# Rotary turning of queries and keys: one projection read twice by VectorE instead of two projections

## The reference, cut to what matters

```python
q, k, v = (heads(wq, bq), heads(wk, bk), heads(wv, bv))   # x @ w.T + b, split into 16 heads of 8
xr, xi = (t[..., :half], t[..., half:])                   # half = 4
q_or_k = jnp.concatenate([xr * cos - xi * sin, xr * sin + xi * cos], axis=-1)
att = softmax(where(causal, q @ k.T / sqrt(8), -inf))
y = (att @ v) @ wp.T + bp
```

## Time and profile before

| | |
|---|---|
| median of 3 runs | 1955.2 us |
| the profiled execution | 1959.13 us |
| its span, first to last instruction | 1957.4 us |
| mean granted TensorE clock | 0.977 of full speed |
| TensorE busy | 1787.4 us (91% of the span) |
| VectorE busy | 1570.6 us (80%) |
| ScalarE busy | 1274.1 us (65%) |
| GpSimd busy | 1049.5 us (54%) |
| chain of waits, by engine | TensorE 54%, VectorE 30%, ScalarE 10% |

### The profile page before, as it was taken

One profiled execution on the slowest core, in us unless ns is written; L12 is line 12 of the kernel. 1 busy time (PEld: TensorE's weight loads), 2 busy tenths in 40 slices (PEclk: granted clock), 3 DMA queues, 4 the chain that ended last, 5 costly groups with the idle time before them and its releaser, 6 DMA issues.

```text
span 1957.4 us, 32660 instructions
## 1 busy us (share of the span) xinstructions
PE 1787.4 (91%) x11328; PEld 894.7 (46%) x11328; DVE 1570.6 (80%) x2936; ACT 1274.1 (65%) x2803; POOL 1049.5 (54%) x1124
## 2 busy tenths in 40 slices
PE   4878999999999999999999999999999999998894
PEld 2343545445454544545455454544545454453443
DVE  6487888889888798988879788887978888797661
ACT  1547577675857768586775857667585766758461
POOL 1416374665637466463746646374664647555533
PEclk8989999999999999999999999999999999999887
DMA  2211011110101111110111111011110101100000
GB/s 78 62 43 33 12 39 39 45 39 31 47 12 40 38 45 39 31 44 15 39 39 45 38 31 36 22 39 39 44 40 31 31 28 39 39 11 21 1 11 6
DMA packets 87361, 66.61 MB, mean 34 GB/s; under 512 B 10592, under 2 KB 82976, under 8 KB 87200
## 3 DMA queue, kind: packets, MB, share of 16 engines
q1 hardware_dynamic: 87200, 64.52, 10.8%
HBM read 30.42 MB, written 8.39 MB: 20 GB/s over the span
## 4 chain that ended last, share of the span: by engine, by line
PE 54%; DVE 30%; ACT 10%; issue 3%; POOL 1%; DMA 1%; SPq 0%; POOLq 0%; PEld 0%; DVEq 0%; PEldq 0%; ACTq 0%
PE Y L494 9%; DVE nmaxA L877 7%; DVE ztmp L992 6%; PE S1c L433 5%; PE S2a L459 4%; PE S1b L433 4%; DVE nmaxF L882 4%; ACT Pq L721 4%; PE S2b L459 4%; PE Y L485 4%; PE M L587 3%; PE M L545 3%; ACT PT L706 3%; DVE ztmp L964 2%; PE M L599 2%
## 5 line engine op out<-in xcount | busy, mean ns | idle before, releaser
L1110 POOL TENSOR_TENSOR Z<-Z,ztmp 128x1280 f32<-128x1280 f32 x112 | 324.6, 2898 | 339.9 <-DVE ztmp L992 338.8
L1077 POOL TENSOR_SCALAR_AFFINE_SELECT PT<-PT 128x256 f32<-128x256 f32 (+1 forms) x640 | 256.3, 410 | 290.9 <-ACT PT L706 285.8
L1101 POOL TENSOR_TENSOR Vf<-Vf,ztmp 128x512 f32<-128x512 f32 x256 | 349.0, 1363 | 94.4 <-DVE ztmp L964 85.8
L706 ACT ACTIVATE PT<-S2a 128x512 f32<-128x512 f32 x320 | 191.8, 599 | 132.5 <-PE S2a L453 126.1
L494 PE MATMUL Y<-PT,Vf 128*64 128x512 f32 x1024 | 267.8, 614 | 0.0
L710 ACT ACTIVATE PT<-S2a 128x512 f32<-128x512 f32 x256 | 153.4, 599 | 151.5 <-PE S2a L459 148.1
L964 DVE TENSOR_TENSOR ztmp<-xv,wv_s 128x512 f32<-128x512 f32 x256 | 240.2, 938 | 2.8 <-POOL Z L1110 2.8
L433 PE MATMUL S1c<-Kf,Qf 64*128 64x512 f32 x352 | 201.8, 654 | 26.8 <-ACT Pq L721 25.7
L433 PE MATMUL S1a<-Kf,Qf 64*128 64x512 f32 x352 | 201.4, 652 | 25.6 <-ACT Pq L721 25.6
L706 ACT ACTIVATE PT<-S2b 128x512 f32<-128x512 f32 x320 | 191.9, 600 | 25.9 <-PE S2b L453 25.6
L433 PE MATMUL S1b<-Kf,Qf 64*128 64x512 f32 x320 | 183.3, 653 | 10.2 <-ACT Pq L721 10.1
(11 more groups left out here) (111 smaller groups left out, 3729.8 us busy)
## 6 DMA issues: line engine op xcount, KB each, us to landing
Qs<-parts SPq DMA_DIRECT2D x96, 128.0 KB
Ks<-parts SPq DMA_DIRECT2D x96, 128.0 KB
tab_s<-in_tab SPq DMA_DIRECT2D x16, 512.0 KB, 4.4
out_x<-res SPq DMA_DIRECT2D x32, 256.0 KB, 2.2
xr<-out_x SPq DMA_DIRECT2D x24, 256.0 KB, 2.9
wa_s<-in_wa SPq DMA_DIRECT2D x16, 320.0 KB, 3.2
xl<-in_x SPq DMA_DIRECT2D x8, 256.0 KB, 3.0
Qs<-mrowA SPq DMA_DIRECT2D x128, 4.0 KB, 1.7
```

What stands on the lines that cost most here:

```text
L706: nc.scalar.activation(PT[:, slot % 2, b, :], t[:, :], ACT.Exp, scale=SCALE_A).then_inc(exps_done.sem, 1)
L1101: nc.gpsimd.tensor_tensor(Vf[:, i, :, :], Vf[:, i, :, :], vtmp[:, n % VBUF, :, :], ALU.add).then_inc(v_acc.sem, 1)
L1110: nc.gpsimd.tensor_tensor(Z[:, :, :, :], Z[:, :, :, :], ztmp[:, hh % 2, :, :, :], ALU.add).then_inc(z_acc.sem, 1)
```

## The change

The second projection of the query and of the key, `A qp` and `A kp`, goes, with its weights, its bias and its places in the list of M0. `wa_s` has 3 blocks of weights instead of 5 (the transfer goes from 320 to 192 KB). For half 1 VectorE reads the one projection again, crosswise: partitions 64 to 127 of the bank are written to partitions 0 to 63 of `rot2`, and 0 to 63 to 64 to 127, in two instructions of 64 partitions and 512 columns each. The sign in the second table moves to the other half, since it is now read on the partition of the source. The bank is given back behind the second of these, and not behind half 0; a new semaphore `turned` counts the other two instructions, and the sum waits for it. The steps stay: half 0 of the query at (2, 6), both crosswise instructions and the sum at (2, 7); of the key at (3, 5) and (3, 6).

```diff
@@ the lists of banks @@
                    "rows2", "F k2", "ZT1", "F out",
-                   "rows3", "A xnT", "A qp",
-                   "A kp", "F k3",
+                   "rows3", "A xnT",
+                   "F k3",
@@ TensorE @@
-                    w = ("A q", "A qp", "A k", "A kp").index(use)
+                    w = ("A q", "A k").index(use)
...
                         if at == (2, 6):
                             a_project("A q")
-                        if at == (2, 7):
-                            a_project("A qp")
                         if at == (3, 4):
                             a_project("A k")
-                            a_project("A kp")
@@ VectorE, rotate(qk, half) @@
-                    use = (("A q", "A qp"), ("A k", "A kp"))[qk][half]
+                    use = ("A q", "A k")[qk]
...
                     dve.wait_ge(*filled(j, use))
-                    nc.vector.scalar_tensor_tensor((rot, rot2)[half], bank(use)[:, :],
-                                                   ba_s[:, 2 * qk + half:2 * qk + half + 1], tab_s[:, half, :],
-                                                   ALU.add, ALU.mult).then_inc(is_free(use), 1)
-                    if half:
-                        for use in (("A q", "A qp"), ("A k", "A kp"))[qk]:
-                            dve.wait_ge(*drained(j, use))
-                        nc.vector.tensor_tensor(rot, rot, rot2, ALU.add).then_inc(rot_ready.sem, 1)
+                    t = bank(use)
+                    if half == 0:
+                        nc.vector.scalar_tensor_tensor(rot, t[:, :], ba_s[:, qk:qk + 1], tab_s[:, 0, :],
+                                                       ALU.add, ALU.mult).then_inc(turned.sem, 1)
+                        return
+
+                    nc.vector.scalar_tensor_tensor(rot2[0:P // 2, :], t[P // 2:P, :], ba_s[P // 2:P, qk:qk + 1],
+                                                   tab_s[P // 2:P, 1, :], ALU.add, ALU.mult).then_inc(turned.sem, 1)
+                    nc.vector.scalar_tensor_tensor(rot2[P // 2:P, :], t[0:P // 2, :], ba_s[0:P // 2, qk:qk + 1],
+                                                   tab_s[0:P // 2, 1, :], ALU.add, ALU.mult).then_inc(is_free(use), 1)
+                    dve.wait_ge(turned.sem, turned.at(j, 2 * qk + 2))
+                    dve.wait_ge(*drained(j, use))
+                    nc.vector.tensor_tensor(rot, rot, rot2, ALU.add).then_inc(rot_ready.sem, 1)
@@ the host @@
-        w = np.stack([wq[:, plain], wq[:, swapped], wk[:, plain], wk[:, swapped], wv], 1)
-        b = np.stack([bq[plain], bq[swapped], bk[plain], bk[swapped]], 1)
+        w = np.stack([wq[:, plain], wk[:, plain], wv], 1)
+        b = np.stack([bq[plain], bk[plain]], 1)
...
-        tabs.append(np.stack([np.repeat(np.concatenate([cos, cos]), H, 0), np.repeat(np.concatenate([-sin, sin]), H, 0)], 1))
+        tabs.append(np.stack([np.repeat(np.concatenate([cos, cos]), H, 0), np.repeat(np.concatenate([sin, -sin]), H, 0)], 1))
```

More of the change, by code:

```diff
@@ L96, in attention_and_mixture @@
         maskb = sb("maskb", [P, P], BF)
-        wa_s = sb("wa_s", [P, 5, C])
+        wa_s = sb("wa_s", [P, 3, C])
         wp_s = sb("wp_s", [P, C])
         bp_s = sb("bp_s", [P, C])
-        ba_s = sb("ba_s", [P, 4])
+        ba_s = sb("ba_s", [P, 2])
         bv_s = sb("bv_s", [P, C])
@@ L226, in attention_and_mixture @@
         rot_ready = Signal("rot_ready", 2)
+        turned = Signal("turned", 4)
         part0_ready = Signal("part0_ready", 2)
@@ L552, in a_project_values @@
                     for i in range(NT):
-                        last = nc.tensor.matmul(t[:, i * C:(i + 1) * C], xnT[:, i * P:(i + 1) * P], wa_s[:, 4, :],
+                        last = nc.tensor.matmul(t[:, i * C:(i + 1) * C], xnT[:, i * P:(i + 1) * P], wa_s[:, 2, :],
                                                 start=True, stop=True)
@@ L809, in _ @@
             for s in (m0_drained, m1_drained, s1_read, maxF_ready, resA_ready, resF_ready, varA_ready, varF_ready, xnA_ready,
-                      xnF_ready, rot_ready, nmb_ready, v_mult, z_mult, lnA_chain, lnF_chain, maxA_chain,
+                      xnF_ready, rot_ready, turned, nmb_ready, v_mult, z_mult, lnA_chain, lnF_chain, maxA_chain,
                       normA_chain, pick_chain, mix_chain):
@@ L1152 @@
     plain = [h * D + d for d in range(D) for h in range(H)]
-    swapped = [h * D + (d + D // 2) % D for d in range(D) for h in range(H)]
     def layout(wq, wk, wv, wp, bq, bk, bv, bp):
-        w = np.stack([wq[:, plain], wq[:, swapped], wk[:, plain], wk[:, swapped], wv], 1)
-        b = np.stack([bq[plain], bq[swapped], bk[plain], bk[swapped]], 1)
+        w = np.stack([wq[:, plain], wk[:, plain], wv], 1)
+        b = np.stack([bq[plain], bk[plain]], 1)
         return w, wp, b, np.broadcast_to(bv, (C, C)), np.broadcast_to(bp, (C, C))
```

## The result

The changed kernel took 1977.7 us (median of 4 runs, 1977.2 to 1979.0) against 1955.1 us before: 22.7 us slower, ratio 1.0117, 95% interval 1.0103 to 1.0131. Slower was forecast, at 1967.2 us; the range ended at 1974.5.

The account below looks back on a forecast made before the run. TensorE (54% of the chain) and VectorE (30%) hand work to each other, neither alone the bound. Steady units +10.9, unit at 964 +0.3, first unit +2.0, second -1.2: +12.0 on 1955.2 gives 1967.2 us, range 1958.5 to 1974.5.

Parts of the forecast that it names:

- Both places read in the steady unit: Query and key turning in the repeating 114.8 us unit: removed matmuls open only 0.61 and 0.31 us, VectorE being next late.
- The price of a half-width instruction: VectorE: 64 partitions cost a full 0.75 us, plus some 0.08 us before starting when the first partition changes.
- The rival without a hold: Changing the first partition costs VectorE nothing; instructions follow at 0.60 and 0.67 us; +4.7 us, 1959.9 us; chance 0.15.
- Place 1 at 0.15 us: Query turning, third group of a unit: sum 0.30 us later, partly covered; middle of 0 and 0.30 taken per unit.
- Place 2 at 0.63 us: Key turning, fourth group of a unit: the sum on VectorE comes 0.63 us later per unit and delays the chain.
- the delayed sum of the earlier trace: Unit at 1308.17 before the change: key's sum 0.35 us late, unit 0.34 us longer, so delay passes on whole.
- The first unit: Both turnings on the start-up chain; each gains an instruction at 0.83 us and loses 0.16 us overlap: +2.0 us together.
- The second unit: VectorE nearly idle, removed matmuls of 1.06 and 0.86 us on TensorE's own chain: -1.2 us.
- What goes: Step counting removed TensorE matmuls: 1.07 us at the query, 0.86 at the key, 27 to 34 us over 32.
- the unit of 115.4 to 115.8 us: Sign to look for in the profile after: a steady unit this long instead of 114.8 us.
- The delay is covered: Rival: the sum is late, but a parallel GpSimd or ScalarE wait is nearly as long; within 4 us; chance 0.08.
- Cheap halves: Rival: a 64-partition instruction takes about half, 0.37 us, so removed matmuls win; -16.6 us, 1938.6 us; chance 0.10.

Follow-up runs that it names:

- the queries alone: The changed kernel with the change kept for the queries only; the keys keep both projections and the 128-partition instruction: 1967.5 us.
- the matmul alone away: The kernel before without the query's second projection; one 128-partition instruction reads the first projection, not crosswise: 1949.3 us, ratio 0.9975.
- the same partitions: The changed kernel with both half-width instructions reading and writing partitions 0 to 63, so no crosswise turning: 1967.6 us.

## Why the prediction was right or wrong

- **Both places read in the steady unit: right.** TensorE's removed work gained nothing, since VectorE was next at both.
- **The price of a half-width instruction: right, a little high.** Full duration for half the partitions, and no overlap where the first partition changes. Forecast distances 0.76 and 0.83 us, measured 0.70 to 0.72 and 0.79: each starts 0.03 to 0.04 us after the end of the one before, not 0.08. The Trainium skill's rule ("VectorE: DVE Perf Modes", section "Two Vector instructions with no wait between them") is borne out by the same two instructions with and without a change of partitions, 0.10 to 0.13 us each. The rival without a hold is out.
- **Place 1 at 0.15 us: too high.** The sum is 0.20 us later, not 0.30, and that costs 0, the lower end: all is covered, as the queries alone show (unit 114.83). It was the first product behind the sum that gave way (0.89 to 0.69 us); the second, on which the argument rested, still took 1.42 us.
- **Place 2 at 0.63 us: measured 0.51**, and it passes on whole, as the delayed sum of the earlier trace rows had it. The sum of these two, 14 x 0.78 = 10.9 us, became 14 x 0.51 = 7.1 us. "F q3" queues (0.80 us), at no cost of its own.
- **The first unit: right.** Each turning took 0.91 us more (forecast 1.0). The second unit and the start together came out at -1.1 us where I had -1.2 + 2.0; the clock falls at other moments there (granted 0.87 of full speed over the first 159 us before, 0.94 over the first 158 after), and I didn't take that apart.
- **The step that failed is "What goes".** It asked what TensorE's missing matmul opens for others and left every other duration in the unit as it was. It never asked what TensorE does in the opened time: it idles, 2.03 us instead of 1.38 at place 1, and the clock falls to its lower level in 13 of the 14 steady units. With a matmul put back there, even unread, the clock stays up and 16.9 us come back. That term, 17.8 us, was left out of the sum without a reason, and it is larger than all of the forecast's 12.0 us. The windows of before would have shown the granted clock at 1.00 over 1493 us of steady units and the start-up with several falls; neither stood in the prediction. So the direction was right for the smaller part of the reasons, and the unit of 115.4 to 115.8 us that I named was nearly met (115.33) only in the one unit where the clock stayed up.
- **The rivals.** *The delay is covered* holds at place 1 alone. *Cheap halves* is out: 0.75 us. None of the three had the clock in it.

What stays open: why, within one kernel and at the same idle times of TensorE, the clock fell in some units and not in others (4 of 14 with the matmul alone away, 9 with the same partitions, 13 in the changed kernel and with the queries alone). The first steady unit of the changed kernel had the same 0.32 and 1.71 us and kept its clock. That is seen, not explained.

## What to carry to other kernels

Before work is taken off TensorE in a loop that runs at the upper clock, look where TensorE will then stand idle, and read the granted clock of those stretches after: here one matmul per unit paid for itself by keeping the clock up, even unread. Here an instruction on half the partitions cost VectorE as much as on all of them, and 0.10 to 0.13 us more where its first partition wasn't that of its forerunner. And ask of each extra piece of work which maximum, or other step on the chain, stands behind it in the engine's order: moving the key's second half and its sum behind one maximum gave 0.70 us per unit, and no correct version with one projection read twice reached that, even with the same move in it (0.45 at best).

## What the runs showed of the hardware that I had not expected

TensorE's clock fell to 1.2 GHz behind idle times that sum to 2.03 us and are broken by matmuls, in a kernel whose TensorE is busy for 90% of the span; with 1.38 or 1.46 us at that place it never did in the traced runs. One fall cost 1.1 us of a unit in the changed kernel, 1.2 and 1.6 us in two of the experiments, and 2.6 us where it lasted twice as long. The falls are not tied to one spread of times: the kernel with the matmul alone away, with 4 falls in its trace, ranged over 7.6 us in ten runs, and so did the kernel before in the thirteen runs beside it, with no fall in its traced steady units; the one with the unread matmul ranged over 1.3 us in six. Each kernel was traced once, so how the number of falls varies from run to run isn't shown.
